# LoRA B in four quarters with homes, banks and queues of their own, and a wait in front of POOL's first x plus bias

## The reference

```python
x = x + _L0_ffn_ref(_L0_cond_ref(x, cond_128, ...), gate, kernel, bias, lora_A, lora_B, lora_A_shared, lora_B_shared)
...
# _L0_cond_ref: per batch a 64 x 64 mixing of channels, chosen by an attention over 8 experts
att = softmax(mlp(cond_128)); agg_w = einsum('bk,koi->boi', att, weight); agg_b = att @ bias_k
out = einsum('boi,bih->boh', agg_w, x) + agg_b[:, :, None]
...
# _L0_ffn_ref: 8 groups of 256 rows, each with LoRA matrices that its gate mixes from 16
base_out = matmul(x, kernel) + bias
A_eff = einsum('bn,nri->bri', gate, lora_A); B_eff = einsum('bn,nor->bor', gate, lora_B)
delta = einsum('bor,btr->bto', B_eff, Ax) + einsum('or,btr->bto', lora_B_shared, Ax_s)
```

## Time and profile before

| | before |
|---|---|
| time, median of 3 runs | 885.17 us (884.15 to 886.46) |
| the profiled execution, own time | 888.03 us |
| its span, first to last instruction | 886.1 us |
| PE busy | 845.3 us (95%) |
| DVE busy | 297.5 us (34%) |
| ACT busy | 134.3 us (15%) |
| POOL busy | 136.4 us (15%) |
| mean granted clock of PE | 0.985 |

### The profile page before, as it was taken

How to read it: one execution, slowest core, us unless ns; L and a number is a source line. 1 busy time by engine, 2 the same in 40 slices (tenths; PEclk the granted TensorE clock), 3 DMA queues, 4 the chain that set the end, 5 groups by cost and what they waited for, 6 DMA issues and landing times.

```text
span 886.1 us, 11052 instructions
## 1 busy us (share of the span) xinstructions
PE 845.3 (95%) x4177; PEld 712.0 (80%) x4177; DVE 297.5 (34%) x365; ACT 134.3 (15%) x179; POOL 136.4 (15%) x75
## 2 busy tenths in 40 slices
PE   5982999999999999999999999999999989999998
PEld 4861888888888899888888888888888868888886
DVE  3753332333231677312121213130305932222221
ACT  3421010101010233301120112010102311100000
POOL 3530323142222000000000000000000312222221
PEclk9996899999999999999999999999999999999999
DMA  8744762555447966002020202020216544444441
GB/s 246 197 134 145 212 165 74 129 134 143 117 122 168 215 144 143 13 24 72 24 71 24 72 24 74 32 71 24 71 39 176 153 131 143 142 142 148 150 149 51
DMA packets 73156, 99.92 MB, mean 113 GB/s; under 512 B 8024, under 2 KB 55560, under 8 KB 72104
## 3 DMA queue, kind: packets, MB, share of 16 engines
q1 hardware_dynamic: 71952, 98.70, 39.8%
q10 hardware_dynamic: 1032, 0.63, 0.2%
q0 software_dynamic: 144, 0.21, 0.1%
HBM read 63.45 MB, written 36.06 MB: 112 GB/s over the span
## 4 chain that ended last, share of the span: by engine, by line
PE 88%; DMA 5%; DVE 4%; SPq 2%; issue 1%; ACT 0%; DVEq 0%; ACTq 0%
PE ps L1117 88%; DMA x<-x_scratch 2%; DVE w_t L979 1%; SPq L357 1%; DMA lora_b_scratch<-lb_c_lo 1%; DVE w_lo L1000 1%; DMA lb<-lora_b_scratch 0%; DVE z L886 0%; DMA raw<-in_L_ffn_w 0%; DMA lora_b_scratch<-lbs_lo 0%; DVE h_lo L1069 0%; DVE lb_c_lo L904 0%; DMA gate_t<-in_L_ffn_gate 0%; SPq L440 0%; PE ps L1169 0%
## 5 line engine op out<-in xcount | busy, mean ns | idle before, releaser
L1117 PE MATMUL ps<-c_hi,w_hi 128*128 128x512 f32 x512 | 199.3, 389 | 0.0
L1117 PE MATMUL ps<-c_hi,w_lo 128*128 128x512 f32 x512 | 199.2, 389 | 0.0
L1117 PE MATMUL ps<-c_lo,w_hi 128*128 128x512 f32 x512 | 199.2, 389 | 0.0
L606 POOL TENSOR_TENSOR res<-x_in,b_s 128x1024 f32<-128x1024 f32 x16 | 51.0, 3193 | 535.1 <-DMA b_s<-in_L_ffn_b 413.9
L1117 PEld LDWEIGHTS ps<-c_hi,w_lo 128*128 128x128 f32 x512 | 96.1, 188 | 20.1
L1117 PEld LDWEIGHTS ps<-c_lo,w_hi 128*128 128x128 f32 x512 | 96.1, 188 | 19.9
L1117 PEld LDWEIGHTS ps<-c_hi,w_hi 128*128 128x128 f32 x512 | 96.1, 188 | 19.8
L1041 DVE SCALAR_TENSOR_TENSOR h_s<-ps,b_s,silu_s 128x512 f32<-128x512 f32 x32 | 24.0, 751 | 248.5 <-PE ps L1117 248.5
L1117 PE MATMUL ps<-w_hi,h_hi 128*128 128x512 f32 x256 | 100.2, 392 | 2.9 <-DVE w_lo L1000 2.9
L1117 PE MATMUL ps<-w_lo,h_hi 128*128 128x512 f32 x256 | 100.3, 392 | 0.0
L1117 PE MATMUL ps<-w_hi,h_lo 128*128 128x512 f32 x256 | 100.3, 392 | 0.0
(11 more groups left out here) (125 smaller groups left out, 741.7 us busy)
## 6 DMA issues: line engine op xcount, KB each, us to landing
raw<-in_L_ffn_w SPq DMA_DIRECT2D x96, 128.0 KB, 3.2
x_scratch<-x_t SPq DMA_DIRECT2D x16, 516.0 KB, 2.7
x_scratch<-x_t SPq DMA_DIRECT2D x128, 64.5 KB, 2.5
x<-x_scratch SPq DMA_DIRECT2D x16, 516.0 KB, 6.4
x_in<-x_scratch SPq DMA_DIRECT2D x16, 516.0 KB, 5.4
x_in<-in_x SPq DMA_DIRECT2D x16, 512.0 KB, 4.2
h_scratch<-h_s SPq DMA_DIRECT2D x32, 256.0 KB, 2.3
h_in<-h_scratch SPq DMA_DIRECT2D x16, 512.0 KB, 4.7
```

The source lines that it names most:

```text
L606: pool.tensor_tensor(res[s][:, :].rearrange("p (b h q) -> p h q b", h=2, q=4), blocks(x1_in[s]), b3_s[:, :].rearrange("p (b h q) -> p h q ...
L1117: return pe.matmul(o, l, r, start=start, stop=stop)
```

## The change

Chunks 2 and 3 of LoRA B get homes of their own (where the taps and `f_bias` will lie) and are loaded and turned first. The four quarters go to banks 6, 7, 0 and 1, all ahead of the last steps of u, and none waits for another. `turn_taps` moves behind u's last step, the load of x tile 2 moves with it, and `z_group(0)` goes behind `y_tile(2)`. The four stores of pair 0 stay on SP's queue, those of pair 1 go to ACT's. The first piece of `y_bias` is half as wide, its matmul and that of `yb_c` stand behind the transposes of the mixing matrices, and `take_z(0)` stands behind `take_y(3)` on DVE. POOL's first "x plus bias" waits for `lb_turned` 4 and for `z_taken` 1.

```diff
-        LA_BANKS, LB_BANKS = (4, 5, 6, 7), (7, 6, 7, 6)
+        LA_BANKS, LB_BANKS = (4, 5, 6, 7), (6, 7, 0, 1)
-        RAW_LBS, RAW_LB = 4, KT + 1
+        RAW_LBS, QUART = 4, HALF // 2
+        LB_ORDER = (2, 3, 0, 1)
-        lb_raw = [at(f"lb_raw{s}", [P, NL], 144.25 + 4 * s) for s in range(2)] + [raw[(RAW_LB + c) % 4] for c in range(2)]
+        lb_raw = [at(f"lb_raw{s}", [P, NL], 144.25 + 4 * s) for s in range(2)] + [at(f"lb_raw{s}", [P, NL], 202.25 - 4 * s) for s in (2, 3)]
...
+        def store_lb(eng, pair):
+            eng.wait_ge(lora_taken, 4 + pair + 3)
+            for hl in range(2):
+                for odd in range(2):
+                    eng.dma_start(lb_w[hl, odd, pair], lb_c[hl][64 * odd:64 * odd + 64, pair, :]).then_inc(lb_stored[pair], 16)
...
+            sp.wait_ge(gate_mm, 1)
+            load_lora_b(2)
+            load_lora_b(3)
             load_raw(RAW_LBS, lora_b_s.rearrange("(b o) r -> b (o r)", b=32), rows=32)
             sp.wait_ge(mix_mm, 4)
             load_lora_b(0)
             load_lora_b(1)
+            store_bias(0, yb_c, yb_stored)
             load_wk(4)
+            load_wk(5)
             store_bias(1, cb_c, cb_stored)
...
             wait_slot(sp, raw_of(KT - 2))
             load_x(3, 3)
...
+            sp.wait_ge(taps_mm, 1)
+            load_x(2, 2)
+            store_lb(sp, 0)
...
             pool.wait_ge(fbias_in, 16)
-            pool.wait_ge(lb_turned, 2)
+            pool.wait_ge(lb_turned, 4)
+            pool.wait_ge(z_taken, 1)
...
+            for n in range(4):
+                lb_hi_part(n)
             act.wait_ge(taps_mm, 1)
...
+            store_lb(act, 1)
...
             dve.wait_ge(mix_mm, 4)
             dve.tensor_copy(mix[0:NC, :, 0:NC].rearrange("p t (c o) -> p t c o", c=4), mix_result(0)).then_inc(mix_made, 1)
+            dve.wait_ge(bias_mm, 1)
+            dve.tensor_copy(yb_c[:, :], bank(0)[0:NB, 256:256 + NC]).then_inc(bias_made, 1)
...
+            for n in range(4):
+                lb_lo_part(n)
+            dve.wait_ge(bias_rest_loaded, 16)
             take_y(2, 1, 0)
             take_y(3, 1, 1)
+            take_z(0, 0, True)
             take_x1(0, 0)
...
+            pe.wait_ge(lora_taken, 4)
+            lb_result_mm(0)
+            lb_result_mm(1)
+            dst, dst1 = first_u(0, 5), first_u(1, 5)
+            lb_result_mm(2)
+            lb_result_mm(3)
+            for k in range(6, 8):
+                dst, dst1 = first_u(0, k), first_u(1, k)
             turn_taps()
-            for k in range(5, 7):
-                dst, dst1 = first_u(0, k), first_u(1, k)
-                if k == 5:
-                    pe.wait_ge(taps_made, 1)
-                    lb_result_mm(0)
-                    lb_result_mm(1)
-            dst, dst1 = first_u(0, 7), first_u(1, 7)
-            pe.wait_ge(lora_taken, 4 + 2)
+            pe.wait_ge(lora_taken, 4 + 4)
+            y_tile(2, 2, 16)
+            pe.wait_ge(taps_made, 1)
             z_group(0, 0, True)
-            lb_result_mm(2)
-            y_tile(2, 2, 16)
-            lb_result_mm(3)
             y_tile(3, 3, 16)
             pe.wait_ge(lb_loaded[0], LB_FIRST)
```

More of the change, by code:

```diff
@@ L126, in layered_kernel @@
         sel = at("sel", [NLORA, P], 190.25)
-        yb_r, ones = at("yb_r", [P, HALF], 155.25), at("ones", [P, P], 157.25)
+        yb_r, ones = at("yb_r", [P, HALF // 2], 155.25), at("ones", [P, P], 157.25)
         las_raw = at("las_raw", [RANK, NL], 186.25)
@@ L318, in store_bias @@
                 sp.dma_start(bias_dram[n].rearrange("(b o) -> b o", o=NC), src[:, :]).then_inc(stored, 16)
-            store_bias(0, yb_c, yb_stored)
             lb_v = lora_b.rearrange("(a n) (c b q) r -> c a b n (q r)", n=4, c=4, b=32)
@@ L333, in _ @@
             load_lora_b(1)
+            store_bias(0, yb_c, yb_stored)
             load_wk(4)
+            load_wk(5)
             store_bias(1, cb_c, cb_stored)
-            for k in range(5, KT):
-                load_wk(k)
-            for c in (2, 3):
-                wait_slot(sp, RAW_LB + c - 2 - 4)
-                load_lora_b(c)
-            sp.wait_ge(taps_mm, 1)
-            load_x(2, 2)
+            load_wk(6)
+            load_wk(7)
             sp.wait_ge(lbs_made, 2)
@@ L665, in _ @@
             wk_hi_part(0)
-            act.wait_ge(yb_mm, 1)
-            act.activation(y_bias[:, 0:HALF], bank(3), ACT.Copy).then_inc(yb_made, 1)
             act.wait_ge(mix_zeroed, 1)
@@ L670, in _ @@
             act.activation(mix[NC:, :, NC:].rearrange("p t (c o) -> p t c o", c=4), mix_result(1), ACT.Copy).then_inc(mix_made, 1)
+            act.wait_ge(yb_mm, 1)
+            act.activation(y_bias[:, 0:QUART], bank(3)[:, 0:QUART], ACT.Copy).then_inc(yb_made, 1)
             wk_hi_part(1)
@@ L686, in _ @@
             wk_hi_part(5)
+            act.wait_ge(lb_turned, 1)
+            with nc.allow_non_contiguous_dma(reason="a few columns of small arrays"):
+                act.dma_start(f_bias[:, :], f0_bias.partition_broadcast(P)).then_inc(fbias_in, 16)
+                act.dma_start(b12_s[:, :, :], b12.rearrange("(h p j) -> p h j", h=2, j=NJ)).then_inc(b12_in, 16)
+            wk_hi_part(6)
+            wk_hi_part(7)
+            act.wait_ge(lbs_stored, 32)
+            for n in range(4):
+                lb_hi_part(n)
             act.wait_ge(taps_mm, 1)
@@ L691, in _ @@
             last.then_inc(taps_made, 1)
-            wk_hi_part(6)
-            act.wait_ge(lbs_stored, 32)
-            lb_hi_part(0)
-            lb_hi_part(1)
-            wk_hi_part(7)
-            with nc.allow_non_contiguous_dma(reason="a few columns of small arrays"):
-                act.dma_start(f_bias[:, :], f0_bias.partition_broadcast(P)).then_inc(fbias_in, 16)
-                act.dma_start(b12_s[:, :, :], b12.rearrange("(h p j) -> p h j", h=2, j=NJ)).then_inc(b12_in, 16)
-            lb_hi_part(2)
-            lb_hi_part(3)
-            with act.Fori(0, 3) as i:
+            store_lb(act, 1)
+            split_y(2, 1, 0)
+            split_y(3, 1, 1)
+            for k in range(4, 6):
+                split_y(k, (k // 2) % 2, k % 2)
+            with act.Fori(1, 3) as i:
                 for k in range(2, 6):
@@ L1153, in _ @@
             pe.wait_ge(att_taken, 1)
-            pe.wait_ge(consts_made, 5)
-            pe.wait_ge(yb_spread, 1)
-            mm(bank(3), ones[:, :], yb_r[:, :], True, True).then_inc(yb_mm, 1)
-            pe.wait_ge(biask_in, 16)
-            mm(bank(0)[0:NB, 256:256 + NC], att_s[:, 0, 0, :], biask_s[:, :], True, True).then_inc(bias_mm, 1)
             pe.wait_ge(expert_in, 16)
@@ L1171, in _ @@
                 last.then_inc(mix_mm, 1)
+            pe.wait_ge(biask_in, 16)
+            pe.wait_ge(consts_made, 5)
+            pe.wait_ge(yb_spread, 1)
+            mm(bank(3)[:, 0:QUART], ones[:, :], yb_r[:, :], True, True).then_inc(yb_mm, 1)
+            mm(bank(0)[0:NB, 256:256 + NC], att_s[:, 0, 0, :], biask_s[:, :], True, True).then_inc(bias_mm, 1)
             def small_turns():
```

46 lines of the change are left out of this document (16 added, 30 removed).

## The result

The changed kernel takes 882.63 us (median of 20 runs, 880.44 to 885.12) against 885.17 (883.54 to 887.05, 20 runs): a ratio of 0.997, interval 0.9962 to 0.9979. On another chip it was 885.24 against 888.03, 0.9966 (0.9953 to 0.9978). So the gain is 2.5 to 3.0 us and not 10.4, and the time lies outside the range of 872.0 to 880.0. The profiled execution took 881.88 us.

The account below looks back on a forecast made before the run. PE was busy for 95% of the span, its one large wait 14.8 us for LoRA B. `y_tile(4)` moving from 96.29 to 85.9 gave -10.4 us: 877.6 from the profiled 888.03, 874.8 against the median 885.17; range 872.0 to 880.0.

Parts of the forecast that it names:

- the pause ahead of `y_tile(2)`: PE idles while x tile 2 loads behind the taps: 3.8 us, and 0.4 for shared DMA engines.
- the step from there to `z_taken`: PE resumes at 61.8, `y_tile(3)` ends at 69.6, DVE's low parts and take_z follow: `z_taken` 1 at 73.6.
- the share of 0.50: While LoRA B's stores flow, half the DMA engines work; a second queue reaches the same half, so nothing is faster.
- the second way: Path to `y_tile(4)` through LoRA B's stores, loads and u_lora: 84.7, just ahead of the other path's 85.9.
- so I keep the 2.6: Front: `y_tile(0)` starts 2.6 us earlier, and this survives the later kernel rows with a margin of 1.5 us.
- I take 73.5: Last landing of LoRA B's eight stores: 57.7 + 16.8 = 74.5, taken as 73.5 because the shared matrix's loads come later.
- From the last landing to the first u_lora it took 4.8: Between LoRA B's last store landing and PE's first u_lora: 4.8 us as before, giving 78.3.
- the slower rival: Two store queues on the same eight DMA engines hinder each other, far below 164 GB/s: about 890 us, chance 0.06.
- The forecast's own sign of being wrong: LoRA B's load as last release of `y_tile(4)`, PE idle before 57 us, or new waits behind 150 us.
- the first way: Path to `y_tile(4)` through `z_taken`, POOL's two adds (7.8 us) and the x load (4.3 us): 85.9, the one that decides.
- -10.4: `y_tile(4)` starts at 85.9 instead of 96.29; the whole 10.4 us is taken off the execution time.
- The wait for z: POOL's adds begin only behind `z_taken` 1, so they no longer run beside `take_z(0)`: buys 3.3 us.

Follow-up runs that it names:

- pool_gap: The changed kernel with POOL's third low part of the kernel matrix held until DVE has made y's low part: 881.66 us, ratio 0.9926 to before.
- taps_early: The changed kernel with the taps turned ahead of LoRA B's quarters again, as before: 877.84 us, ratio 0.9869 to before.
- taps_gap: The changed kernel with the edits of taps_early and pool_gap joined: 875.81 us, ratio 0.9858 to before.
- taps_gap_queue: taps_gap with all eight stores of LoRA B on SP's queue: 874.37 us, ratio 0.9829 to before.
- one_queue: The changed kernel with pair 1's stores on SP's queue behind those of pair 0, as before: 881.42 us, ratio 0.9928 to before.
- wide_store: one_queue with LoRA B stored by four DMAs of 128 rows and each group read back by four DMAs: 883.56 us, ratio 0.9943 to before.
- wide_wait: all_four with POOL's wait for the first z put back: 877.16 us, ratio 0.9875 to before.
- all_four: The changed kernel with the edits of taps_early, pool_gap and wide_store, and without POOL's wait for the first z: 873.98 us, ratio 0.9833 to before.

## Why the prediction was wrong, point by point

**Right.** The order of the front up to `y_tile(0)` (17.51 to 18.70, forecast 17.8); the pause ahead of `y_tile(2)` (3.8 us and 0.4 for shared DMA engines forecast, 3.80 measured) and the low clock behind it (`y_tile(2)` took 3.76 us); the wait for `wk_lo` gone; the step from there to `z_taken` (the adds begin at 76.07, forecast 73.6, and the difference is what the front gave back); POOL's two adds at 7.51 us; the share of 0.50 with both queues. The Trainium skill's rule in "DMA: Bandwidth & Descriptors", section "Issuing engines are not separate DMA queues", holds here: a second issuer opened no second half. Stores of another shape did (share 1.00 at 364 GB/s), which agrees with the same page's section "Why a DMA increments its semaphore by 16 and not by 1": the number of engines in use follows from the slowest dimension of the transfer's two sides.

**Wrong, three terms of the second way**, the one through LoRA B. Forecast it was 57.6 + 15.9 + 4.8 + 6.4 = 84.7; measured, 60.05 + 17.78 + 7.10 + 5.77 = 90.70.
- *"so I keep the 2.6"* failed: 2.5 us. The step watched DMA, the kernel rows 4 to 7, and these were in time. What took the gain back was POOL beside DVE at 20 to 26 us, which pool_gap and the kernels after it show, and in the first and third execution the low clock that followed. Some 0.8 us of the 2.6 was never there: the execution that it was counted from is the one with the late `y_tile(0)`. In the first execution nearly all of the 2.6 is lost (the taps end at 60.05), in the luckiest of the five 0.7 (58.26).
- *"I take 73.5"* for the last landing: 1.9 us too short on its own count (17.8 for 15.9 from the end of the taps). It took the time of one queue for two. In one queue the eight stores take 15.0 us here; in two, 17.4. With early taps the two queues took 18.1 and 15.9 us (taps_early, taps_gap) and one 16.4 (taps_gap_queue), so that two are slower is seen in the change's place only, and why stays open.
- *"From the last landing to the first u_lora it took 4.8"* failed: 7.10. Before, the first pair is out well ahead of the second and the loads of the shared matrix lie beside the second's flight. Now both queues start within 0.4 us of each other and share the 0.50, pair 0 lands no earlier than 77.83, and those loads stand in the path: 77.83 to 84.93, and 6.9 to 7.3 us in the other four executions. One_queue shows it: 75.67 to 80.00, 4.3 us. So do taps_early and taps_gap, where SP starts 1.1 us ahead: 4.9 and 5.2 us.
- u_lora and z took 5.77 instead of 6.4, the one term in the change's favour.

The forecast named the place of the slower rival (two queues that hinder each other), but only with a price so high that it had to be slower than before. A smaller price of the same mechanism, 4.2 us with both terms, was enough to make this way the longer one, and no case had it. The forecast's own sign of being wrong came true: PE's last wait ahead of `y_tile(4)` is the one for LoRA B's load, 13.1 us where 6 to 9 were forecast, and the short one for x isn't there.

**Wrong, the first way as the bound.** POOL's adds end at 83.58, and a load of 4.3 us puts x at about 88, while PE is busy with LoRA B's work until 90.70. Of the kernels run here, this way bounds only where LoRA B is faster: in one_queue by 0.47 us, in wide_store by 3.93, in wide_wait by 3.88.

**The last step, "-10.4" carried over to the time "against the median".** The failures above alone would have given 885.17 - 5.5 = 879.7, still inside the range; what puts the time outside is this step. Even the measured start of `y_tile(4)`, 5.5 us earlier in the mean, isn't in the median: 4.2 in the spans of the profiled executions, 2.5 to 3.0 in the timed ones. 1.3 us are the low stretches behind the mark. That the change meets these more often than before is seen in three of five against none of three, and chance isn't excluded. The remaining 1.2 to 1.7 us stay open: timed executions don't show where the clock was low, and the profiled ones come from several chips, on which the median of before alone runs from 885.2 to 888.7 us.

**The wait for z.** In the forecast it bought 3.3 us off the path and cost 1.2, since the way through it ended at 85.9 and the other at 84.7. In the change it buys nothing and costs nothing (0.9957 without it, 0.9966 with it). It costs where LoRA B's way is shorter (wide_wait against all_four).

**The change's own choices.** LoRA B's quarters ahead of the taps cost most: 8.6 us by the ratio of taps_early. What the marks show of it is the start of the stores, 3.3 us earlier, and of `y_tile(4)`, 3.0 us earlier. The pause of 3.8 us and the low clock behind it are the plainest thing to see and aren't shown to cost anything: a wait of 13 us for LoRA B follows on PE, which takes up whatever is saved ahead of it. The rest of the 8.6 us stays open. The best kernels here, taps_gap_queue and all_four, are 14 to 15 us faster than before and by the ratios 12 faster than the change.

## What to carry to other kernels

When work on an engine is moved earlier, look up what runs beside it at its new place, on VectorE and GpSimd above all: a pair of subtractions that took 1.5 to 3.0 us before took 5.0 to 5.1 in four of five executions. When transfers are spread over a second queue, ask whether the queue or the DMA engines were full, and when the *first* of them will be out, since something is waiting for it. And when a start on the busiest engine moves, count the clock behind it too: a pause closed in one place and opened just ahead of the next dense stretch gave its gain back. Last, count a saving only on the chain that ends last: a pause with a longer wait behind it on the same engine costs nothing, as long as that wait doesn't hang on the work that the pause puts off.
